# A sixth of the front's convolution on TensorE, the front's turn in another order, and 64-row products in the recurrence, in a two-layer transformer kernel

## The reference

```python
q = short_conv(x @ Wq, conv_q); k = short_conv(x @ Wk, conv_k); v = short_conv(x @ Wv, conv_v)
q = mix * apply_rotary(q, sin, cos) + (1.0 - mix) * q          # k likewise
beta = sigmoid(x @ Wb); gamma = sigmoid(x @ Wgamma)
# delta_rule_chunkwise, per head, for chunks of 32 rows:
T = inverse of (1 + strictly lower part of kb @ k.T); u = T @ v; w = T @ kb
def step(S, xs):
    attn = qi @ ki.T * tril_inc
    u_t = ui - wi @ S
    o_i = qi @ S + attn @ u_t
    S_new = g * S + ki.T @ u_t
core = rmsnorm(o, o_norm_w) @ Wo
frac = rmsnorm(fractal_mixer(x, frac_conv_w), mixer_norm_w)    # shifts by 1, 2, 4, 8
x = x + ga * (core + sigmoid(x @ frac_gate_w + frac_gate_b) * frac)
h = layernorm(x) * (1 + cb) + sb
x = x + gb * (int8-quantised rows of h @ weight_q * scales + bias)
```

## Time and profile before

| | us |
|---|---|
| median of 3 runs | 3015.98 (3015.29 to 3019.74) |
| profiled execution | 3019.29 |
| its span, and what lies around it | 3017.5, 1.8 |
| mean granted TensorE clock | 0.924 of full |

### The profile page before, as it was taken

How to read it: one execution, slowest core, us unless ns; L and a number is a source line. 1 busy time by engine, 2 the same in 40 slices (tenths; PEclk the granted TensorE clock), 3 DMA queues, 4 the chain that set the end, 5 groups by cost and what they waited for, 6 DMA issues and landing times. The chain is left out here.

```text
span 3017.5 us, 92586 instructions
## 1 busy us (share of the span) xinstructions
PE 2653.1 (88%) x35848; PEld 1615.2 (54%) x35848; DVE 2272.8 (75%) x4387; ACT 1593.9 (53%) x2172; POOL 293.7 (10%) x292
## 2 busy tenths in 40 slices
PE   6879999899989998999999978999987787209997
PEld 3322466666655765667556624555545565206774
DVE  3449899789979897999889914556557888685776
ACT  2320677677767776777667773111116776304442
POOL 1246000000000000000000020000000000002333
PEclk9985899999999999999999988999998988659998
DMA  4253011101110111101110001000001232413442
GB/s 138 80 107 73 3 27 28 26 6 27 27 28 5 26 26 28 23 9 27 27 27 6 5 12 58 14 28 14 14 6 29 78 97 88 125 30 108 114 111 65
DMA packets 155981, 133.47 MB, mean 44 GB/s; under 512 B 101762, under 2 KB 133124, under 8 KB 150404
## 3 DMA queue, kind: packets, MB, share of 16 engines
q1 hardware_dynamic: 149892, 124.08, 17.5%
q10 hardware_dynamic: 4224, 4.19, 0.4%
q0 software_dynamic: 1536, 0.40, 0.1%
HBM read 81.56 MB, written 46.66 MB: 42 GB/s over the span
## 5 line engine op out<-in xcount | busy, mean ns | idle before, releaser
L697 DVE TENSOR_REDUCE attn_pm<-attn_MS 128x1 f32<-128x512 f32 (+3 forms) x2304 | 1334.1, 638 | 174.5 <-PE attn_MS L741 147.6
L681 ACT ACTIVATE attn_PT<-attn_ES 128x1024 f32<-128x1024 f32 (+5 forms) x1152 | 1039.1, 951 | 375.8 <-PE attn_ES L776 373.1
L791 PE MATMUL attn_OP<-attn_PT,attn_VH 128*17 128x512 f32 (+3 forms) x4608 | 653.6, 564 | 0.2 <-ACT attn_PT L681 0.2
L741 PE MATMUL attn_MS<-head_KX,head_QX 96*32 96x512 bf16 (+11 forms) x3456 | 395.2, 393 | 5.8 <-DVE attn_pm L697 3.5
L741 PE MATMUL attn_MS<-after_attention,attn_QX 96*32 96x512 bf16 (+8 forms) x2880 | 339.2, 359 | 4.1 <-issue 3.0
L776 PE MATMUL attn_ES<-head_QX,head_KX 99*32 99x512 bf16 (+6 forms) x3456 | 287.6, 369 | 42.0 <-issue 20.9
L741 PE MATMUL attn_MS<-attn_KX,attn_QX 96*32 96x512 bf16 (+7 forms) x2880 | 318.0, 371 | 1.3 <-DVE attn_pm L697 1.1
L776 PE MATMUL attn_ES<-attn_QX,attn_KX 99*32 99x512 bf16 (+9 forms) x2880 | 248.4, 358 | 5.1 <-ACT attn_PT L681 4.4
L776 PE MATMUL attn_ES<-attn_QX,after_attention 99*32 99x512 bf16 (+10 forms) x2880 | 242.2, 359 | 4.6 <-ACT attn_PT L681 4.3
L1180 PE MATMUL l0out_ring<-l0out_w,l0out_sT 128*128 128x512 f32 x512 | 225.0, 592 | 0.0
L741 PEld LDWEIGHTS attn_MS<-head_KX,head_QX 96*32 96x32 bf16 x3456 | 155.1, 97 | 123.8 <-DVE attn_pm L697 60.2
(11 more groups left out here) (289 smaller groups left out, 3495.8 us busy)
## 6 DMA issues: line engine op xcount, KB each, us to landing
vk_beta<-front_vk SPq DMA_DIRECT2D x8, 1024.0 KB, 4.0
kq_transposed<-l0out_w_in SPq DMA_DIRECT2D x8, 1024.0 KB, 4.7
delta_VK<-vk_beta SPq DMA_DIRECT2D x32, 256.0 KB, 2.8
delta_QK<-kq_transposed SPq DMA_DIRECT2D x32, 256.0 KB, 2.9
attn_QX<-qk_parts SPq DMA_DIRECT2D x60, 128.0 KB, 7.4
head_KX<-qk_parts SPq DMA_DIRECT2D x36, 128.0 KB, 6.5
head_QX<-qk_parts SPq DMA_DIRECT2D x36, 128.0 KB, 7.2
after_attention<-attn_out SPq DMA_DIRECT2D x18, 256.0 KB
```

The costliest lines, as they stand in the source:

```text
L681: nc.scalar.activation(PT[u % NPT][:, 512 - wa:512 + wb], ES[half][:, 512 - wa:512 + wb], ACT.Exp, scale=DH ** -0.5).then_inc(exp_done, 1)
L697: nc.vector.tensor_reduce(pm[r][:, i, c:c + 1], MS[slot][:, 0:w], AX.X, ALU.max).then_inc(max_taken, 1)
L741: last = nc.tensor.matmul(MS[slot][r, 0:seen], QX[b][0:ROWS, i * P + 32 * g:i * P + 32 * g + 32], KX[b][0:ROWS, 512 * c:512 * c + seen], s ...
L791: last = nc.tensor.matmul(OP[32 * j:32 * j + DH + 1, 512 - w:512], VH[b][:, kt, :], PT[(2 * n + half) % NPT][:, o:o + w], start=(kt == 0), ...
```

## The change

It has three parts.

**A.** The load of the mask stands at the start of `project`. Behind the store of each part of each group, SP copies head 0's rows of that part from the buffer in SBUF straight into `head_KX` and `head_QX`: 6, 4 and 2 copies for `hi`, `mid`, `lo`, 96 in all. The buffers wait for these too. The 12 loads from DRAM are gone.

**B.** Block 5 of the front's convolution goes to PE: four products with diagonal matrices of the taps (`conv5`, made by DVE once) into `nat`, behind `rates` and ahead of `mix`; its scaled copy on ACT and its three steps on DVE are gone, and its silu reads `nat`. PE's order in a turn becomes: blocks 2 and 3, heads 0 and 1, block 4, heads 2 and 3, block 5, `rates`, the new products, `mix`; ACT's is changed the same way. `turn_heads` writes `nat` and `tp` in turn, so it waits for the copy before the last.

**C.** In the recurrence `f_mt` and `f_b` become eight products each, with 64 rows and 128 columns, in the free halves of two banks of `atp`, which is three banks now; `mtp` is gone. `f_mt` also waits for DVE's mask of its tile. The gates move from POOL to ACT (eight activations a tile), the modulation from POOL into DVE's `normalise` (four scalar_tensor_tensor for two tensor_scalar), and DVE's and PE's orders change: `f_at(2i+1)` ahead of the second `t_s`, the statistics behind it, `f_at(2i+2)` right behind the scaled rows, and PE's `turn_heads` ahead of `f_mt(2i+2)`.

```diff
@@ project, sync
+            sp.dma_start(head.mask[:], d["c_mask"].rearrange("a p n -> p a n")).then_inc(head.mask_in, 16)
...
                 sp.dma_start(qk_out[0][:, :, cols], hi[:]).then_inc(hi_out, 16)
+                head.load_group(sp, 0, hi, cols, hi_out)
...
-            head.load(sp, 0, head.KX, head.QX, head.loaded)
+            sp.sem_inc(head.loaded, 12 * 16)
@@ class FirstHead
+    def load_group(self, sp, p, part, cols, landed):
+        for r in range(6):
+            if KPARTS[r] == p:
+                sp.dma_start(self.KX[DH * r:DH * r + DH, cols], part[0:DH, 2, :]).then_inc(landed, 16)
+            if QPARTS[r] == p:
+                sp.dma_start(self.QX[DH * r:DH * r + DH, cols], part[0:DH, 0, :]).then_inc(landed, 16)
@@ layer1_front, scalar
-                nc.scalar.activation(acc[:, 0, m, :], pr[:, m % 2, :], ACT.Copy, scale=cw[:, m, TAPS - 1:TAPS])
+                if m < 5:
+                    nc.scalar.activation(acc[:, 0, m, :], pr[:, m % 2, :], ACT.Copy, scale=cw[:, m, TAPS - 1:TAPS])
                 nc.scalar.activation(pre[:, m, 3:], pr[:, m % 2, :], ACT.Copy).then_inc(aad, 1)
...
                 act.wait_ge(bmd, BM(g - 1, "nat_3"))
-                nc.scalar.activation(qkv[:, m, :], acc[:, 1, m, :], ACT.Silu).then_inc(aad, 1)
+                nc.scalar.activation(qkv[:, m, :], acc[:, 1, m, :] if m < 5 else nat[:], ACT.Silu).then_inc(aad, 1)
@@ layer1_front, vector
+            for t in range(TAPS):
+                last = nc.vector.tensor_scalar(conv5[:, t, :], k["ident"][:], cw[:, 5, t:t + 1], None, ALU.mult)
...
-                    for m in (a, a + 1):
+                    for m in (a, a + 1) if a < 4 else (a,):
@@ layer1_front, tensor
+            def convolve_last(g, heads):
+                pe.wait_ge(aad, AA(g, "pre_5"))
+                if heads:
+                    pe.wait_ge(bad, BA(g - 1, "X_2"))
+                for t in range(TAPS):
+                    last = nc.tensor.matmul(nat[:], conv5[:, t, :], pre[:, 5, t:t + 512],
+                                            start=(t == 0), stop=(t == TAPS - 1))
+                last.then_inc(amd, 1)
...
-                if j:
-                    pe.wait_ge(bad, BA(g, f"X_{j - 1}"))
                 if j >= 2:
+                    pe.wait_ge(bad, BA(g, f"X_{j - 2}"))
                     pe.wait_ge(bvd, BV(g, f"vb_{j - 2}"))
@@ recurrence, scalar
+            def gates(t, b):
+                act.wait_ge(df, DF(t - 2, "MT"))
+                act.sem_inc(aheld, 1)
+                for a in range(2):
+                    for c in range(CT):
+                        last = nc.scalar.activation(gI[b][:, a, c, :], id64[:], ACT.Copy,
+                                                    scale=gall[:, bass.ds(t * CT * 2 + 2 * c + a, 1)])
+                last.then_inc(gi, 1)
@@ recurrence, vector
                 for j in range(U):
-                    last = nc.vector.tensor_scalar(xn[:, j, :], xt[:, j, :], mv[:, j, 0:1], rs[:, j:j + 1],
-                                                   ALU.subtract, ALU.mult)
+                    last = nc.vector.scalar_tensor_tensor(xn[:, j, :], xt[:, j, :], mv[:, j, 0:1], k["cb1"][:],
+                                                          ALU.subtract, ALU.mult)
                 last.then_inc(v2, 1)
+                dve.wait_ge(v2, V2(n, "xn"))
+                for j in range(U):
+                    last = nc.vector.scalar_tensor_tensor(h4[:, j, :], xn[:, j, :], rs[:, j:j + 1], k["sb1"][:],
+                                                          ALU.mult, ALU.add)
+                last.then_inc(v2, 1)
@@ recurrence, tensor
             def f_mt(t, b):
                 pe.wait_ge(af, AF_(t, "UW"))
+                pe.wait_ge(df, DF(t, "atm"))
+                pe.sem_inc(theld, 1)
                 for h in range(HB):
                     r = slice(DK * (h % 2), DK * (h % 2) + DK)
-                    o = (h // 2) * 2 * P
-                    last = nc.tensor.matmul(mtp[r, o:o + 2 * P], UW[b][:, h, DK:], KBD[b][:, h, :, :],
-                                            start=True, stop=True)
+                    o = (h // 2) * P
+                    for s in range(2):
+                        own = slice(2 * C * s, 2 * C * s + 2 * C)
+                        last = nc.tensor.matmul(steps_p[r, s, o:o + P], UW[b][own, h, DK:],
+                                                KBD[b][own, h, 2 * s:2 * s + 2, :], start=True, stop=True)
                 last.then_inc(mf, 1)
```

More of the change, by code:

```diff
@@ L200, in project @@
     M = Steps("qk_0", "qk_1", "qk_2", "qk_3", "vh_0", "vh_1", "vh_2", "vh_3")
+    HI, MID, LO = (16 + 16 * n for n in head.of_part)
     with ExitStack() as st:
@@ L560, in attention @@
         held = sem("pool_held")
-        mask_in, ready = sem("mask_in"), sem("attn_ready")
+        mask_in, ready = head.mask_in, sem("attn_ready")
         loaded = [head.loaded] + [sem(f"qk_loaded{b}") for b in range(1, NB)]
@@ L1440, in turn @@
             def turn(n, b, zero, one, two):
-                for m in range(4):
+                for half in range(2):
+                    if one:
+                        for m in ((2, 3), (4,))[half]:
+                            take_projection(n - 1, m)
                     if two:
-                        take_heads(n - 2, m)
-                    if two and m == J - 1:
-                        own_share(n - 2)
-                    if one:
-                        for p in ((2, 3), (), (4,), (5,))[m]:
-                            take_projection(n - 1, p)
+                        for j in (2 * half, 2 * half + 1):
+                            take_heads(n - 2, j)
+                if one:
+                    take_projection(n - 1, 5)
+                if two:
+                    own_share(n - 2)
                 if one:
@@ L1775, in turn @@
             def turn(n, b, zero, one, two):
-                for m in range(4):
+                for half in range(2):
+                    if one:
+                        for m in ((2, 3), (4,))[half]:
+                            project(n - 1, 1 - b, m)
                     if two:
-                        turn_heads(n - 2, m)
-                    if one:
-                        for p in ((2, 3), (), (4,), (5,))[m]:
-                            project(n - 1, 1 - b, p)
+                        for j in (2 * half, 2 * half + 1):
+                            turn_heads(n - 2, j)
                 if one:
+                    project(n - 1, 1 - b, 5)
                     rates(n - 1, 1 - b)
+                    convolve_last(n - 1, two)
                     mix(n - 1, 1 - b)
                 if zero:
-                    turn_over(n)
+                    turn_over(n, two)
                 if two:
@@ L2021, in _ @@
-            turn(NU + 2, False, False, True)
+            pool.sem_inc(o3, O3.primed)
+            pool.wait_ge(wready, 2)
+            for n in range(1):
+                residual_and_bias(n)
+            with pool.Fori(1, NU) as n:
+                residual_and_bias(n)
         @block.scalar
@@ L2097, in _ @@
             turn(1, True, True, True, False)
-            turn(2, True, True, True, True)
-            with act.Fori(3, NU - 1) as i:
+            with act.Fori(2, NU - 1) as i:
                 turn(i, True, True, True, True)
@@ L2285, in turn @@
                 if three:
-                    output(i - 3)
+                    scaled_rows(i - 3)
+                if second:
+                    f_at(2 * i + 2, 0)
                 if first:
                     t_s(2 * i + 1, 1, 1)
-                if second:
-                    f_at(2 * i + 2, 0)
+                if three:
+                    output(i - 3)
                 if first:
@@ L2365, in f_b @@
                 pe.wait_ge(df, DF(t, "MT"))
+                pe.sem_inc(theld, 1)
                 for h in range(HB):
                     r = slice(DK * (h % 2), DK * (h % 2) + DK)
-                    o = (h // 2) * 2 * P
-                    last = nc.tensor.matmul(bp[r, o:o + 2 * P], KN[b][:, h, :], UBD[b][:, h, :, :],
-                                            start=True, stop=True)
+                    o = (h // 2) * P
+                    for s in range(2):
+                        own = slice(2 * C * s, 2 * C * s + 2 * C)
+                        last = nc.tensor.matmul(steps_p[r, s, o:o + P], KN[b][own, h, :],
+                                                UBD[b][own, h, 2 * s:2 * s + 2, :], start=True, stop=True)
                 last.then_inc(mf, 1)
```

122 lines of the change are left out of this document (56 added, 66 removed).

## The result

The changed kernel takes 2985.06 us (median of 4, 2975.98 to 2991.01) where the kernel before takes 3016.73 (the three executions above and one more); the ratio is 0.9895, with a 95% interval of 0.988 to 0.9909, so 31.7 us less (27 to 36). The forecast was 46 less. It is faster, and inside the range, but a third of the forecast gain is missing. The profiled execution took 2985.76 us with a span of 2983.9, 33.6 under the span before.

The account below looks back on a forecast made before the run. Limits taken: DVE at attention start, DVE's chain in a front turn, PE in the recurrence. 3019.29 - 10.3 - 28.5 - 7.4 = 2973.1, less 3.3 to the median, written 2969.5 us; range 2956 to 2991.

Parts of the forecast that it names:

- Part A, -10.3: Attention start: first maximum at 206.8 to 207.3 instead of 217.59, 10.3 us less (9 to 11).
- An issue takes 0.46 us: End of `project`: SP's last 15 copies, begun at 193.72, end near 200.7 and land at 203.7, ahead of DVE's 204.70.
- Part B, -28.5: Front: steady turns of 36.5 instead of 41.08 us, summed over all turns to 28.5 us less (range -20 to -33).
- The margin of 0.7: Front turn: `mix` ends at 24.5, ACT's squares need it at 25.2; it fits by 0.7 us, costed at nothing.
- next late is ACT: Front turn, squares to first copied projection: ACT takes 12.2 us, DVE's own way 11.3; ACT could hold the turn by 0.9.
- rival 1: Front: ACT and PE hold the turn, `mix` late or clock falling; turn 37.5, front -20 to -22, about 2977; chance 0.20.
- Part C, -7.4: Recurrence: 0.4 us less a pair, 3.0 less in the first three turns, 0.8 more in the tail (-15 to +6).
- rival 2: Recurrence: 64-row records spaced by width, 1.18 to 1.30 us a product, total 2996 to 3003; chance 0.10, midway 0.12.
- The stall: Recurrence pair: PE waits some 0.9 us before the even tile's `f_mt` and 0.15 at the odd tile, for DVE.
- first three turns -3.0: Start of the recurrence: the first three turns together take 3.0 us less.
- rival 3: Recurrence: a 64-row record costs 0.1275 us, a product 2.04; +75 us, total +36 or 3052; chance 0.04.
- rival 4: Attention start: copies land late or something else holds the first maximum; -1 to -5 instead of -10.3, 2976; chance 0.06.

Follow-up runs that it names:

- part C alone: The kernel before with only the recurrence part of the diff: ratio 0.9991 (0.9981 to 1.0001), 2.7 us less.
- norm_late: The changed kernel with DVE's head norms and scaled rows ahead of the odd tile's first step, the normalise later: 2977.05 us, 0.9865.

## Why the prediction was right or wrong

**Part A, -10.3; shown -5.9 at its place (-6.5 from DVE's last work on), timed alone -7.5 (-11 to -4).** Two steps failed. "An issue takes 0.46 us": the copies from SBUF take 0.6 to 0.7 each, so the last are issued at 204.8 and land behind DVE's end, not at 203.7 ahead of it; the block starts 1.35 behind DVE and not 0.40. And "the cast comes 0 to 0.5 later, the way from cast to first maximum is unchanged": I had looked for who *waits* for POOL's memsets, and no one does; that DVE's cast beside one lasts as long as the memset was not in the sum. Before, the mask arrived as the last memset ended (at 216.06; the cast begins at 215.96), so the trace of before could not show it:

```profile
212.55 3.51 POOL L619 MEMSET after_attention<- 3x4096 bf16 x1
```

The slack in the loop was as said: ACT's write of `hi` in the second group stands at 64.12, 63.88 before.

**Part B, -28.5; shown -25.3.** The first turn costs +2.99 (2.95 forecast), the turns 3 to 7 are 35.9 to 37.3, which are just the bounds that were given: the upper two, turns 3 and 4, end in or start right behind a stretch with PE at 1.2 GHz. The terms that were mis-sized are turn 2 (-0.4 instead of -2.05: its three instructions were worth little there, and nothing in the kernel with the products alone, where it is 1.0 longer), the last two (-6.3 instead of -7.2), and turns 3 and 4 (-4.2 and -4.0 instead of -4.6 each, the clock); turns 5 to 7 gave 0.4 more than forecast. What was wrong in the working, though the sum hides it, is that -2.0 for the instructions and -2.6 for the waits were added as if each stood alone. The order with the alternating banks gives 21 of the 25; the products without it cost 7. The margin of 0.7 by which `mix` comes in time is one that the new order makes; in the old one it is missed by 0.9, and "next late is ACT" comes true at once: that kernel is rival 1. Of the changed kernel rival 1 is true only in the clock of some turns.

**Part C, -7.4; shown +1.8, timed alone -2.7 (-5.7 to +0.3).** The price of a 64-row product was right: 0.63 was taken, 0.60 measured, and 0.46 to 0.48 ahead of a `rec`. The 16 records over four quarters of the array are 0.0375 apart, so the row of the 64x64 form was the one to go by. The Trainium skill ("TensorE: Matmul & The Clock Gate", Back-to-back issue gap) gives about 81 ns a product at 128 columns for a stream of weight loads and products. An estimate from it for 16 records would be 1.30, the upper end of rival 2, and no run shows it. The 0.074 of the 128x64 form is near 81 ns; the 0.0375 measured is not, so the figure doesn't hold for these small tiles side by side. The stall was forecast at 0.9 + 0.15 and measured at 0.69 + 0.24. The pair is 16.40 instead of 16.85, since two of the four products are followed by a `rec` and cost less. The failed step is "first three turns -3.0": 1.0 a turn, where the loop was to gain 0.4, and no row was given for it. In place of this, part C brings gaps put down to issue, behind the longest of which the granted clock falls: +8.8 in four turns in this trace, +2.6 with part C alone. Why PE runs short there is open. And the tail is +2.0, not +0.8, with the longer normalise named as its cause; the kernel with the short one again still takes 29.8 there, and the kernels without part C take 28.3 to 29.4, so that is not shown to be it.

Rivals 2, 3 and 4: the products of 1.18 to 1.30 and of 2.04 us were not seen; part A did what it says but for 4.4 us, which is rival 4 in part.

## What to carry to other kernels

When a change takes work from an engine and also reorders it, try each alone: in this front the saved instructions were worth nothing, or less, until the order had made room for what replaced them. Ask of a second engine not only who waits for it, but what runs beside it. And when a moved step lands in a chain, look for the slot in which its engine is idle: the same work, placed a few microseconds later, took 0.36 us off each pair, and the gates, moved likewise, another 0.42 (all three moves together with the memsets: 17 us of the total).

## What the runs showed of the hardware that I had not expected

- A DVE cast of 128x256 took 3.62 us beside a POOL memset of 3.51 us, and 0.29 without it; DVE's memset took 0.82 with a POOL memset beside it and without. DVE's head norms took 1.03 where they began during POOL's multiplication, 0.69 without POOL, and 0.69 where they ran beside POOL's addition.
- 16 matmul records of 64x64 with 128 columns take 0.60 us, while 8 of 128x64 with 128 columns take 0.59: the half tiles cost half each.
- DMA issues of 16-row copies from SBUF to SBUF were 0.6 to 0.7 us apart on SP, those of 16-row loads from DRAM 0.46.
- With part C, PE stands still up to 2.4 us at a time in the written-out turns, with no semaphore to wait for that the profile shows, and in the loop of the changed kernel once, for 0.5 (in that of `norm_late` once, for 0.8); the granted clock falls to 0.50 behind such a gap in some of the kernels (0.87 to 1.00 over the first 70 us).
